# The context's inverse deviations go through a DRAM row instead of a TensorE broadcast, and the order around them changes

## The reference

```python
x = L0_attn_x                                   # 16 x 1024 x 256
n = layernorm(x)
phi = cumsum((n @ W_omega.T + b_omega) * exp(log_scale) / sqrt(position))
cm_real, cm_imag = n * cos(phi), n * sin(phi)
mem_real, mem_imag = cumsum(cm_real) / position, cumsum(cm_imag) / position
ret_real = mem_real * cos(phi) + mem_imag * sin(phi)
ret_imag = mem_imag * cos(phi) - mem_real * sin(phi)
context = concatenate([cm_real, cm_imag, ret_real, ret_imag])     # 1024 wide
h = gelu((layernorm(context) * ln_gamma + ln_beta) @ W1.T + b1)    # 512 wide
x = x + n + (h @ W2.T + b2)
x = x + relu(layernorm(x) @ Wq1.T + f_b1) @ Wq2.T + f_b2          # Wq: signs, 1024 wide
```

## Time and profile before

| | |
|---|---|
| runs of the kernel before | 1516.14, 1516.18, 1516.83 us |
| median | 1516.18 us |
| the profiled execution | 1516.45 us, its span 1514.6 us |
| TensorE busy (PE) | 1469.5 us, 97% of the span |
| VectorE busy (DVE) | 1407.4 us, 93% |
| ScalarE busy (ACT) | 1255.5 us, 83% |
| GpSimd busy (POOL) | 558.6 us, 37% |
| chain of waits, by engine | PE 90%, DVE 4%, ACT 2%, issue 2%, DMA 1% |

### The profile page before, as it was taken

How to read it: one execution, slowest core, us unless ns; L and a number is a source line. 1 busy time by engine, 2 the same in 40 slices (tenths; PEclk the granted TensorE clock), 3 DMA queues, 4 the chain that set the end, 5 groups by cost and what they waited for, 6 DMA issues and landing times.

```text
span 1514.6 us, 29961 instructions
## 1 busy us (share of the span) xinstructions
PE 1469.5 (97%) x10685; PEld 880.5 (58%) x10685; DVE 1407.4 (93%) x2325; ACT 1255.5 (83%) x1773; POOL 558.6 (37%) x393
## 2 busy tenths in 40 slices
PE   4789999999999999999999999999999999999998
PEld 3446556656555665656665655666655566565566
DVE  6999999999999999999999999999999999999844
ACT  6769888888888888888888888888888888888756
POOL 1233444432444433344433344444234443334321
PEclk9899999999999999999999999999999999999999
DMA  6445656655756665665665675666576566566542
GB/s 222 78 87 115 124 92 121 126 118 118 139 104 103 123 119 120 132 120 92 125 125 115 123 136 96 111 126 119 115 137 114 96 126 118 120 126 116 91 87 43
DMA packets 236035, 174.98 MB, mean 116 GB/s; under 512 B 139120, under 2 KB 222064, under 8 KB 235888
## 3 DMA queue, kind: packets, MB, share of 16 engines
q0 software_dynamic: 63984, 100.15, 40.5%
q1 hardware_dynamic: 170272, 69.25, 18.8%
q10 hardware_dynamic: 1632, 3.67, 0.7%
HBM read 24.13 MB, written 33.03 MB: 38 GB/s over the span
## 4 chain that ended last, share of the span: by engine, by line
PE 90%; DVE 4%; ACT 2%; issue 2%; DMA 1%; SPq 0%; POOL 0%; DVEq 0%; ACTq 0%; POOLq 0%
PE ps L983 41%; PE ps L1017 15%; PE ps L1004 14%; PE ps L1038 11%; PE ps L939 5%; PE ps L952 3%; DMA ri<-qb 1%; PE ps L965 1%; PE ps L958 0%; DVE ph L1263 0%; SPq L445 0%; DMA lscale<-in_L_attn_log_scale 0%; DVE mr L1311 0%; DVE mi L1297 0%; ACT xs L610 0%
## 5 line engine op out<-in xcount | busy, mean ns | idle before, releaser
L983 PE MATMUL ps<-arena,w_hi 128*128 128x512 f16 x2048 | 609.0, 379 | 0.6 <-DVE arena L1358 0.6
L983 PE MATMUL ps<-arena,w_lo 128*128 128x512 f16 x1024 | 388.1, 379 | 0.0
L983 PEld LDWEIGHTS ps<-arena,w_hi 128*128 128x128 f16 x2048 | 197.8, 98 | 221.8 <-issue 2.0
L1017 PE MATMUL ps<-fw_t,arena 128*128 128x256 f16 x2048 | 254.8, 272 | 1.9 <-DVE arena L1426 1.9
L1004 PE MATMUL ps<-turned,fw_t 128*128 128x512 f16 x1024 | 247.1, 379 | 0.6 <-issue 0.4
L1017 PEld LDWEIGHTS ps<-fw_t,arena 128*128 128x128 f16 x2048 | 195.7, 97 | 69.1 <-issue 30.1
L713 ACT ACTIVATE arena<-ps,relu_bias,relu_scale 128x512 f32<-128x512 f32 x256 | 197.0, 769 | 24.3 <-PE ps L1004 24.0
L1426 DVE TENSOR_TENSOR arena<-arena 128x512 f16<-128x512 f32 x256 | 172.5, 683 | 40.6 <-ACT arena L722 37.2
L1038 PE MATMUL ps<-w_hi,arena 128*128 128x256 f16 x1024 | 174.5, 274 | 4.8 <-DVE arena L1387 4.5
L983 PEld LDWEIGHTS ps<-arena,w_lo 128*128 128x128 f16 x1024 | 100.1, 98 | 120.8
L722 ACT CAST arena<-arena 128x512 f16<-128x512 f32 x256 | 154.5, 615 | 4.3
(11 more groups left out here) (189 smaller groups left out, 2745.1 us busy)
## 6 DMA issues: line engine op xcount, KB each, us to landing
x_rows<-in_L_attn_x SPq DMA_DIRECT2D x32, 512.0 KB, 4.7
rr<-qa POOLq DMA_DIRECT2D x32, 512.0 KB, 7.9
ri<-qb POOLq DMA_DIRECT2D x32, 512.0 KB, 8.4
sqr<-turn POOLq DMA_DIRECT2D x32, 512.0 KB, 5.6
base<-bias_rows POOLq DMA_DIRECT2D x32, 512.0 KB, 5.5
x<-bias_rows POOLq DMA_DIRECT2D x32, 512.0 KB, 5.7
out<-x SPq DMA_DIRECT2D x31, 512.0 KB, 5.7
out<-x POOLq DMA_DIRECT2D x31, 512.0 KB, 6.3
```

What stands on the lines that cost most here:

```text
L983: last = pe.matmul(ps[:, 4 + m], w[:, k, m * P:(m + 1) * P], a[:, c.b, k], start=(i == 0), stop=(i == len(passes) - 1))
L1017: last = pe.matmul(ps_rows_a[:, j], a[:, m % SLOTS, j * P:(j + 1) * P], fw2_t[:, m], start=(m == 0 and j % 2 == 0 and a is rh), stop=(m == ...
```

## The change

Five things change, the first two of which belong together.

- `spread` on TensorE and `spread_out` on ScalarE go. In their place ScalarE issues two DMAs: `deviations_out` writes `crs` to a row of 512 floats in DRAM (`rstd_rows`, one row per parity, one element of 4 bytes at a time), and `deviations_in`, after that DMA's semaphore, reads the row into all 128 partitions of `rb`. `scale_hidden` waits for the second DMA. GpSimd's `inverse_std_context` waits for the earlier write, and TensorE's `omega` and the last `mixer_out` no longer wait for `rb`.
- The orders of VectorE and ScalarE are written anew around this. VectorE makes `first_rows_lo`, `memory_real` and `retrieve_imag_cos` ahead of all four `scale_hidden`, and `second_lo` ahead of `modulate_real` and `context_variance`. ScalarE makes `second_hi` ahead of the cosine, and `relu(now, 0)` between the first and the second gelu, `relu(now, 1)` behind two gelus and two high parts.
- `hidden(nxt, 0)` waits for each quarter of the context where it is used, not for all at its head.
- The signs of the second feed-forward matrix are made in step 0, not in step -1, and the last four of its groups are turned behind `hidden` 2 and 3. The thresholds are computed earlier in the preparation.
- At the very end the last two feed-forward units are summed tile by tile (`last_tiles`), and each half of the output waits for its own tiles.

The core of the diff:

```diff
             def inverse_std_context(c):
                 need(pool, cve_done, c)
-                need(pool, spread_done, c, 1)
+                need_sum(pool, row_done, c, 1)
...
-            def spread_out(c):
-                need(act, spread_done, c)
+            def deviations_out(c):
+                need(act, crs_done, c)
+                act.dma_start(rstd_rows[c.b].rearrange("(t p) -> p t", p=P), crs[:, :],
+                              allow_slow_non_contiguous=True).then_inc(row_done, 16)
+
+            def deviations_in(c):
+                need_sum(act, row_done, c)
                 need(act, z_done[KE - 1], c, 1)
-                act.copy(rb[:, :], ps[:, 2]).then_inc(rbs_done, 1)
+                act.dma_start(rb[:, :], rstd_rows[c.b].partition_broadcast(P)).then_inc(rbs_done, 16)
...
                 if ahead:
                     modulated_hi(ahead)
+                if nxt:
+                    deviations_out(nxt)
                 if far:
                     first_rows_hi(far)
                 if nxt:
-                    spread_out(nxt)
+                    deviations_in(nxt)
...
+                if nxt:
                     gelu(nxt, 0)
...
+                if now:
+                    relu(now, 0)
+                    relu_hi(now, 0)
+                if nxt:
                     gelu(nxt, 1)
                     gelu(nxt, 2)
                     gelu_hi(nxt, 0)
                     gelu_hi(nxt, 1)
                 if now:
-                    relu(now, 0)
-                    relu_hi(now, 0)
+                    relu(now, 1)
+                    relu_hi(now, 1)
...
-            def spread(c):
-                need(pe, crs_done, c)
-                for j in range(NT):
-                    last = pe.transpose(ps[:, 2, j * P:(j + 1) * P], crs[:, j:j + 1].to_broadcast([P, P]), ident[:, :])
-                last.then_inc(spread_done, 1)
...
             def scale_hidden(c, m):
                 need(dve, w1_done[m], c)
-                need(dve, rbs_done, c)
+                need_sum(dve, rbs_done, c)
...
             def output(c):
-                need_block(dve, f2_done, KF - 1, c)
+
                 need_dma(dve, x1_biased, c)
                 for half in range(2):
+                    dve.wait_ge(tile_done, 2 * half + 2)
...
+                if now and now.index == 0:
+                    dve.wait_ge(p_fw2, 16)
+                    dve.wait_ge(p_tern, 2)
+                    signs(1, fw2_in, fw2_signs)
```

More of the change, by code:

```diff
@@ L729, in last_mixer @@
                 second_hi(now)
[L730 removed]
+                deviations_out(last)
+                deviations_in(last)
                 for m in range(KE - 1):
@@ L794, in step @@
                 if nxt:
-                    spread_out(nxt)
-                    gelu(nxt, 0)
+                    deviations_in(nxt)
+                if now and now.index == 0:
+                    for n in SIGN_GROUPS[4:6]:
+                        group_hi(n)
+                if nxt:
+                    gelu(nxt, 0)
+                if now and now.index == 0:
+                    for n in SIGN_GROUPS[6:]:
+                        group_hi(n)
+                if now:
+                    relu(now, 0)
+                    relu_hi(now, 0)
+                if nxt:
                     gelu(nxt, 1)
@@ L1072, in step @@
                             turn_signs(n)
-                    spread(nxt)
+                    if now and now.index == 0:
+                        for n in SIGN_GROUPS[4:6]:
+                            turn_signs(n)
                     hidden(nxt, 3)
+                    if now and now.index == 0:
+                        for n in SIGN_GROUPS[6:]:
+                            turn_signs(n)
                     if not now:
@@ L1087, in step @@
                             ffn_out(now, m - LAG)
-                    for m in range(KF - LAG, KF):
+                    for m in range(KF - LAG, KF if nxt else KF - 2):
                         ffn_out(now, m)
@@ L1091, in step @@
                             last_transposes(nxt)
+                    if not nxt:
+                        last_tiles(now)
                     return
@@ L1480, in step @@
                     gains_1(far)
+                if now and now.index > 0:
+                    second_lo(now)
                 if ahead:
@@ L1485, in step @@
                     context_variance(nxt)
-                if now:
+                if now and now.index == 0:
                     second_lo(now)
@@ L1494, in step @@
                     carry_real(ahead)
+                if far:
+                    first_rows_lo(far)
+                if ahead:
+                    memory_real(ahead)
+                if ahead:
+                    retrieve_imag_cos(ahead)
                 if nxt:
@@ L1498, in step @@
                     scale_hidden(nxt, 2)
-                if far:
-                    first_rows_lo(far)
-                if ahead:
-                    memory_real(ahead)
-                    retrieve_imag_cos(ahead)
                 if nxt:
@@ L1533, in step @@
                     gelu_lo(nxt, 2)
-                    gelu_lo(nxt, 3)
                 if now:
                     relu_lo(now, 4)
+                if nxt and now:
+                    gelu_lo(nxt, 3)
                 if ahead:
@@ L1685, in _ @@
             dve.tensor_scalar(thr[:, :], thr[:, :], 0.5, None, ALU.mult).then_inc(p_thr, 1)
+            context_lo(first, 3, ri[:, :, :])
+            phase_turns(second)
+            phase_sums(second)
+            carry_phase(second)
             prepared(dve)
```

66 lines of the change are left out of this document (30 added, 36 removed).

## The result

| | before | after |
|---|---|---|
| median | 1516.44 us (four runs, 1516.14 to 1516.83) | 1943.86 us (four runs, 1941.87 to 1947.11) |
| ratio | | 1.2819, 95% interval 1.2803 to 1.2835 |
| span of the profiled execution | 1514.6 us | 1943.8 us |
| distance from one in0 to the next, steps 0 to 29 | 44.85 us | 58.46 us |
| mean granted clock of TensorE | 0.991 | 0.899 |

Two executions among the experiments were of a slow state and enter no comparison: 2281.17 us of the orders alone, whose median is 1655.87 without it and not the 1658.6 that some later expectations name, and 3889.13 us of the row with its values 64 bytes apart, which leaves that run one execution.

What follows compares the result with a forecast made beforehand. TensorE was taken to set the 44.85 us step, VectorE close behind; VectorE's new loop of 46.84 plus a row 0.65 late gives 47.49. With 132.65 to step 0, 29 steps and the end: 1597 us, range 1567 to 1648.

Steps and rivals of the forecast that it cites:

- Sum 5.55, bounds 4.4 and 8.9: Row's write to DRAM plus read back: 5.55 us against 4.9 available, so the row is 0.65 us late each step.
- term for the write: Deviations to DRAM: 3.05 us, the middle of a plain store's 2.2 and an element-wise load's 3.9.
- term for the read: Row from DRAM into 128 partitions: 2.5 us, the median of transposes flying then; bounds 2.2 and 3.9.
- VectorE's 3.58: Three operations moved ahead of VectorE's scaled units: 3.58 us, added to its loop from one feed-forward start to the next.
- The transposes: Four broadcast transposes leaving TensorE's queue: a gain of 0.44 us a step while TensorE sets the pace.
- ScalarE's order: Two gelus and high parts ahead of relu 1: TensorE stands 2.04 us at its second feed-forward output group every step.
- The clock: Rival, chance 0.07: TensorE's new pauses bring half clock, at most 0.5 us a step, 1611 us.
- The signs: Sign making moved into step 0: its feed-forward starts 2.5 us later, at 132.65; bounds 0 and 6.1.
- The end: After step 29's feed-forward start: 2.0 us more than before; step 30 hides the row, the final tiles return some tenths.
- the loops and the pause at relu 1: Step loops: TensorE 46.44 us including a 2.04 pause awaiting relu 1, VectorE 46.84, 47.49 with the late row.
- The second rival: Row much later: 4.0 us late, step 50.8, 1695 us; half of that, 1637; chance 0.14 for 1620 to 1695.
- The 2.0 and 2.6 us: Skill-based estimates for the row's two DMAs, fixed cost plus bytes over bandwidth; by these the row would be in time.

Runs made afterwards that it cites:

- the orders alone: Changed kernel with the broadcast by TensorE and the copy by ScalarE as in the kernel before, so only queue orders and smaller edits differ: 1655.87 us.
- the scaled units first: Against the orders alone: VectorE takes scaled units 0 to 2 ahead of first_rows_lo, memory_real and retrieve_imag_cos again; ScalarE's new order stays: 1607.94 us.
- the last kernel with a row: Changed kernel with the row written as 128 runs of 16 bytes and GpSimd's product held until VectorE finished memory_real and retrieve_imag_cos: 1613.12 us.

## Why the prediction was wrong

The step that failed is the price of the row's two DMAs, "Sum 5.55, bounds 4.4 and 8.9". Its term for the write, 3.05 with bounds of 2.2 and 5.0, measured 9.4, and its term for the read, 2.5, measured 5.8. The prediction itself had said that two DMAs outside of 4.4 to 8.9 us would show it wrong.

The miss, 1944 against 1597, adds up from three places: the step (58.46 instead of 47.49, 29 times: 318 us), in0 of step 0 (152.47 instead of 132.65: 20) and the end (96.0 instead of 85.8 from in0 of step 29: 10).

- **The step, along the prediction's path of the row.** In the mean of the 29 steps the product behind relu remainder 1 starts 7.93 after in0 (forecast 7.11; in the rows above 980.28 - 972.34), the deviations stand 33.65 later (33.72), the two DMAs take 15.90 (5.55), the hand-overs 0.13 (0.3), and from the first unit to the next in0 it is 0.84 (0.83). That is 58.46. So of the 10.97 us that the step is longer 10.35 are the DMAs, and 0.8 is in0's matmuls at half clock.
- **The write** was taken as "the middle of 2.2 and 3.9", from a large store and from loads of 256 elements of 4 bytes. The loads are reads from DRAM; the write puts its 512 pieces beside each other into DRAM. The rows at hand did not bound it: the cost is not in the number of pieces alone, by which I scaled. The read, 2.5 in my sum, lands in 3.2 to 3.7 where the write is quick or absent, so it was short by itself too, and in 5.8 behind the slow write; why it is slower there is not shown.
- **VectorE's 3.58** for the three operations is wrong as well, but costs the changed kernel's step nothing, since VectorE stands 9.10 us waiting behind them. They kept their durations of before in my sum, and in the new place `memory_real` meets GpSimd's product and takes 3.37, 2.15 more. Where the row is quick or gone this sets the step: moving GpSimd's product took 1.9 of it out again (48.71 in the quick steps of the orders alone, 46.81 without the collision).
- **The transposes** give 0.43 where I had 0.44. Right.
- **ScalarE's order**: the pause of 2.04 at out1 was right (1.97 and 1.98 with the scaled units first and in the last kernel with a row; 1.13 in the changed kernel's row above, since there half clock stretches in0 to out1 itself).
- **The clock** I had as a rival at 0.07 and at most half a microsecond a step, because the row's loop would give it room. With pauses of 2 us it came in 15 of 29 steps of one kernel, 0.87 a step in the mean, and in 4 of 29 of another. In steps 1 to 29 of the changed kernel, behind pauses of 9.5 to 12.6 us, in0's first sixteen matmuls took 4.9 to 6.6 us instead of 3.62. And that has no room: relu 0 waits for these matmuls, so the row's own path starts 0.8 later. I had one pause of 1.64 with the clock at 1.00 behind it and let it stand for all.
- **The signs**: I had 2.5 us at in0 of step 0. About 5 it is where no row is in the way (135.40 against 130.15), 7 with the row's values 512 bytes apart (137.44). In the changed kernel it is 22, since ScalarE, which copies the turned signs out, stands in the second issue behind the write, and TensorE behind ScalarE, once in step -1 and once in step 0:

```profile
PE ps L1160 <- ACT fw_t L867: 21.1, 2, 14.7
...
152.47 5.63 PE L1014 MATMUL ps<-turned,fw_t 128*128 128x512 f16 x16 [3.62 <-DVE arena L1408]
```

- **The end**: I had step 30 hide the row behind its gelu remainders. VectorE waits there 15.4 us for it.

With the write in 128 runs and the product out of the way the step is 47.83 against 47.49 and the time 1613 against 1597. There the product starts 7.09 after in0 (7.11), out1 comes 7.32 after in0 (7.34), and the row is 0.73 us late in the step shown against my 0.65. So the skeleton of the sum, the loops and the pause at relu 1, held. That the totals come so near is partly luck: the write takes 2.1 there against my 3.05 and the read 3.8 against my 2.5, in the mean, and the two errors cancel in 5.9 against 5.55.

The second rival, a row much later, was the right one in kind and stopped at 1695, because it went by the same rows. The 2.0 and 2.6 us that the prediction worked out from the Trainium skill, page "DMA: Bandwidth & Descriptors", section "Anatomy of one DMA", bound nothing here: that section gives its figures for DMAs that GpSimd issues, the row's two are ScalarE's, and they took 9.4 and 5.8.

What stays open: what happens between the last piece sent and the landing when pieces of 4 bytes are neighbours in DRAM, which no record shows, and what decides whether the clock falls behind a pause of 2 us.

## What to carry to other kernels

Before a small tensor is sent through DRAM, look at how its pieces lie there and not only at how many there are, and bound the landing by a row that goes in the same direction and has its pieces laid out alike. An operation of VectorE that is moved keeps its duration only if its new neighbour on GpSimd lets it: look at what that engine does at the new place. And ask what stands behind an issue that waits for another DMA: here it stood on ScalarE, in a step ahead of gelus that waited for the row anyway, but at the start ahead of the copies of the signs, for which TensorE waited 21 us. No run here put it on another queue.

## What the runs showed of the hardware

- 512 writes of 4 bytes, 2 KB in all: 9.4 us from issue to landing as neighbours in DRAM, 2.7 when 64 or 512 bytes apart, 2.1 as 128 runs of 16 bytes. The pieces go out within 2.1 us of the issue in the first two cases alike, and the landing comes 7.6 us behind the last of neighbours and 0.6 to 0.7 behind the last of pieces apart. While the slow write was under way other DMAs were slow too: transposes 6.5 instead of 2.5 to 4.1 in the runs without it. GpSimd's transfers, issued at other times of the step, were not (`rr` 4.6 us with the slow write and with the one of 512 bytes). In the stretch 961 to 963 above the DMA engines count as more than busy (1.17) and move 49 GB/s.
- Two float32 products of 128 x 1024, one on VectorE and one on GpSimd, run one after the other and not side by side, whichever comes first: 3.37 to 3.44 us for the one that waits, where alone they take 1.22 and 2.36.
- Behind pauses of 1.97 and 1.98 us TensorE's clock was once at its lower level of 1.2 GHz for some four microseconds and once not, at 1.69 us a step between the two. The same pause brought it down in 15 of 29 steps of one kernel and in 4 of 29 of another.
- The same multiplication with one operand read at a stride of 16 bytes takes 1.07 us instead of 0.68.
